# Causal attention and a top-2 expert layer: score products of two heads in the two 64-row halves of the array, and expert weights loaded early

## The reference

```python
def lora_linear(x, w, b, la, lb):
    return x @ w.T + b + 0.5 * (x @ la.T @ lb.T)
# x: (4, 512, 128), 16 heads of 8 channels, all in float32
q, k, v = split(lora_linear(x, w_attn, b_attn, la_attn, lb_attn), 3)
att = softmax(where(causal, q @ k.T / sqrt(8), -inf))          # per head
x = layernorm(x + lora_linear(att @ v, w_proj, b_proj, la_proj, lb_proj))
scores = softmax(x @ router_w)                                # 8 experts
weights, idx = top_k(scores, 2); weights /= sum(weights)
expert_e(x) = (silu(x @ gate[e]) * (x @ up[e])) @ down[e]      # 128 -> 352 -> 128
x = layernorm(x + sum_k weights[k] * expert_idx[k](x))
```

## Time and profile before

| what | us |
|---|---|
| median of 3 runs | 393.46 (392.91 to 393.8) |
| span of the profiled execution, first to last instruction | 388.3 |
| TensorE / VectorE / ScalarE / GpSimd busy | 293.4 / 233.5 / 157.7 / 184.8 |
| first row maxima (L805) | 44.9 |
| first T unit | 57.4 |
| T unit t0 of quads 1 and 2 | 68.4 and 79.8 |
| loop of three passes | 79.8 to 214.7 |
| last score product | 230 |
| first expert product (L1263) | 264.6 |

### The profile page before, as it was taken

The page is one execution under the profiler, slowest core; times in us unless marked ns, Lnnn a source line. Parts: engine busy times, 40 slices in busy tenths (PEclk is TensorE's granted clock), DMA queues, the critical chain, the costliest instruction groups (busy, mean ns, idle before and its releaser), DMA issues.

```text
span 388.3 us, 7846 instructions
## 1 busy us (share of the span) xinstructions
PE 293.4 (76%) x2082; PEld 175.3 (45%) x2101; DVE 233.5 (60%) x561; ACT 157.7 (41%) x258; POOL 184.8 (48%) x291
## 2 busy tenths in 40 slices
PE   2948568979997999989998783208999999999100
PEld 1524323424454445434455332205777777777100
DVE  7699986546687666776677203613545454555082
ACT  1324105546554566636666660011333333333014
POOL 8998623223354475446745722250444443444362
PEclk9988898989999899989999997556999999999755
DMA  6029968908100000000000129442111111111253
GB/s 148 11 101 212 254 119 292 163 4 142 26 3 3 15 29 15 1 0 22 29 8 1 31 56 356 110 117 55 40 51 58 42 49 49 54 50 38 83 145 103
DMA packets 36007, 29.97 MB, mean 77 GB/s; under 512 B 4093, under 2 KB 33920, under 8 KB 35985
## 3 DMA queue, kind: packets, MB, share of 16 engines
q1 hardware_dynamic: 32624, 24.71, 26.6%
q0 software_dynamic: 2304, 4.24, 3.2%
q10 hardware_dynamic: 1056, 0.75, 0.9%
HBM read 16.86 MB, written 13.09 MB: 77 GB/s over the span
## 4 chain that ended last, share of the span: by engine, by line
PE 53%; DVE 16%; issue 8%; DMA 7%; SPq 5%; POOL 5%; ACT 4%; POOLq 0%; ACTq 0%; DVEq 0%
PE slot L1263 13%; PE pvo L1093 7%; PE pvo L1277 7%; PE slot L1071 6%; PE slot L1054 6%; PE slot L1269 3%; SPq L353 2%; PE slot L1050 2%; DMA Qs<-mT 2%; SPq L329 2%; PE misc L1101 2%; ACT pvs L632 2%; DVE negm L805 2%; POOL rows_scratch L527 2%; DMA bqk<-in_L_attn_b_attn_dram 2%
## 5 line engine op out<-in xcount | busy, mean ns | idle before, releaser
L805 DVE TENSOR_REDUCE negm<-slot 128x2 f32<-128x1024 f32 (+2 forms) x96 | 98.8, 1041 | 44.1 <-PE slot L1054 42.4
L659 ACT ACTIVATE Pt<-slot 128x1024 f32<-128x1024 f32 (+1 forms) x96 | 84.5, 880 | 74.2 <-PE slot L1071 71.6
L503 POOL TENSOR_SCALAR_AFFINE_SELECT Pt<-Pt 128x512 f32<-128x512 f32 x56 | 35.5, 634 | 72.8 <-ACT Pt L659 72.4
L575 POOL DMA_INDIRECT chosen_scratch<-Pt x39 | 38.3, 983 | 65.8 <-ACT Pt L712 64.5
L1054 PE MATMUL slot<-Ks,Qs 128*128 (+4 forms) x254 | 57.6, 309 | 1.1 <-DVE negm L805 0.3
L1071 PE MATMUL slot<-Qs,Ks 128*128 (+4 forms) x256 | 53.0, 310 | 5.5 <-DMA Qs<-mT 4.1
L1263 PE MATMUL slot<-Ks,Pt 128*128 x156 | 54.9, 476 | 0.0
L1093 PE MATMUL pvo<-Pt,vst 128*9 128x128 f32 (+3 forms) x512 | 47.4, 450 | 0.0
L1050 PE MATMUL slot<-maskb,identb 128*128 128x128 bf16 (+1 forms) x162 | 38.8, 240 | 6.5 <-DVE negm L805 3.2
L959 DVE COPY Pt<-slot 128x256 f32<-128x256 f32 x39 | 16.5, 424 | 43.2 <-PE slot L1269 43.2
L527 POOL DMA_INDIRECT rows_scratch<-early,place x32 | 31.8, 993 | 15.2 <-issue 8.1
(11 more groups left out here) (164 smaller groups left out, 378.9 us busy)
## 6 DMA issues: line engine op xcount, KB each, us to landing
Qs<-parts_scratch SPq DMA_DIRECT2D x8, 384.0 KB, 5.9
Ks<-parts_scratch SPq DMA_DIRECT2D x8, 384.0 KB, 8.8
Pt<-rows_scratch SPq DMA_DIRECT2D x39, 65.0 KB, 1.8
Qs<-chosen_scratch SPq DMA_DIRECT2D x8, 256.0 KB, 4.9
parts_scratch<-Pt SPq DMA_DIRECT2D x4, 384.0 KB, 6.0
parts_scratch<-early SPq DMA_DIRECT2D x4, 384.0 KB, 3.2
Ks<-in_L_ffn_gate_proj_dram SPq DMA_DIRECT2D x1, 1408.0 KB, 6.8
Ks<-in_L_ffn_up_proj_dram SPq DMA_DIRECT2D x1, 1408.0 KB, 10.0
```

Of the source, the lines that this page charges most:

```text
L503: pool.affine_select(out=v, in_=v, compare_op=ALU.is_ge, fill=0.0, base=0, pattern=[[0, HQ], [1, P]], channel_multiplier=-1).then_inc(sele ...
L575: pool.indirect_dma_start(chosen_scratch, bass.IndirectOffsetOnAxis(xg[:, ring, C:C + 1].bitcast(U32), 0), ys[:, ring % OUT_RING, :], None ...
L659: act.activation(p_view(par, kb)[:, h0:h0 + heads, :], t_view(u, (2 * u + 1) % 3), ACT.Exp, scale=SCALE).then_inc(exp_done, 1)
L805: dve.tensor_reduce(negm[:, par, qb, h0:h0 + heads], s_view(u, n), AX_X, ALU.max, negate=True).then_inc(max_done, 1)
```

## The change

Score products contract one half of the array: 48 rows for S units, 51 for T units, starting at row 0 or 64. `Ks` gets the shape of `Qs`, two heads in one block, without zeros. The maxima and the ones move behind the 48 rows. In a slot, the first half of the columns (one PSUM bank) now belongs to the even heads and the second to the odd ones (`s_view`, `t_view`), so that products issued in turn for rows 0 and 64 write to different banks. The maxima and exponentials address the heads accordingly.

The mask is now made of half-height pieces too: `pick` selects the upper or the lower 64 output rows, `tri` and `tri_after` are the triangles; four products per unit, two of full and two of half block width. Their lower halves are copied by two DMAs on GpSimd's queue. The clearing of the stacks goes on both engines; the ones come by two DMAs of SyncE after the stack of batch 0.

As `Ks` is half as large, `GUW` and `DW` have memory of their own. Their five loads move from SyncE, behind the last score product, to ScalarE, behind the projections' copies and ahead of the first copy of `mT`. `vst` and its copies go; value products read `V9`. TensorE's loop over batches is written out, which makes g a constant.

```diff
 
+
+    ROWS = D * PRODUCTS
+    ALL_ROWS = ROWS + PARTS
     Q_SLOTS = ((0, 3, 0), (3, 2, 1), (5, 1, 2))
...
         onesb = sb("onesb", [P, P], BF16)
-        maskb = sb("maskb", [P, HQ, P], BF16)
-        mask_after = sb("mask_after", [P, HQ, P], BF16)
-        blank_k = sb("blank_k", [P, 2, T], BF16)
-        blank_q = sb("blank_q", [P, T], BF16)
+
+
+        pick = sb("pick", [P, 3 * HALF], BF16)
+        tri = sb("tri", [P, P], BF16)
+        tri_after = sb("tri_after", [P, P], BF16)
+        ones_rows = sb("ones_rows", [PARTS, QPB * 2 * T], BF16)
         PW = [(TB - kb) * P for kb in range(TB)]
         POFF = [HQ * sum(PW[:kb]) for kb in range(TB)]
         Pt = sb("Pt", [P, 2, HQ * sum(PW)])
...
 
-        free_k = Ks[:, :, :, :].rearrange("p g h t -> p (g h t)").bitcast(F32)
-        GUW = free_k[:, 0:2 * E * F].rearrange("p (e w f) -> p e w f", e=E, w=2)
-        DW = free_k[:, 2 * E * F:2 * E * F + E * NFC * C].rearrange("p (e k c) -> p e k c", e=E, k=NFC)
+        GUW = sb("GUW", [P, E, 2, F])
+        DW = sb("DW", [P, E, NFC, C])
         taken = [0]
 
...
-            return slot[n][:, :].rearrange("p (h k) -> p h k", k=[128, 256, 512, 512][qb])[:, 0:heads, 0:(qb + 1) * P]
+            return slot[n][:, :].rearrange("p (a c k) -> p a c k", a=2, k=[128, 256, 512, 512][qb])[:, :, 0:heads // 2, 0:(qb + 1) * P]
 
         def t_view(u, n):
             kb, _, heads = T_UNITS[u]
-            return slot[n][:, :].rearrange("p (h k) -> p h k", k=[512, 512, 256, 128][kb])[:, 0:heads, 0:PW[kb]]
+            return slot[n][:, :].rearrange("p (a c k) -> p a c k", a=2, k=[512, 512, 256, 128][kb])[:, :, 0:heads // 2, 0:PW[kb]]
 
         def p_view(par, kb):
             return Pt[:, par, POFF[kb]:POFF[kb] + HQ * PW[kb]].rearrange("p (h q) -> p h q", h=HQ)
...
 
-                sp.wait_ge(blanked[b], 1)
                 for s in range(2):
                     sp.wait_ge(parts_stored[s][b], 16 * PARTS)
                     src = parts_scratch[b, s].rearrange("(j a r) t -> a r j t", a=2, r=D * PRODUCTS)
                     for a in range(2):
-                        row = HALF * a + PARTS
-                        if s == 0:
-                            dst = Qs[row:row + D * PRODUCTS, QPB * b:QPB * (b + 1)].rearrange("p g c t -> p (g c) t")
-                        else:
-                            dst = Ks[row:row + D * PRODUCTS, QPB * b:QPB * (b + 1)].rearrange("p g (c a) t -> p a (g c) t", a=2)[:, a]
-                        sp.dma_start(dst, src[a]).then_inc(stacks_loaded, 16)
+                        stack = (Qs, Ks)[s][HALF * a:HALF * a + ROWS, QPB * b:QPB * (b + 1)].rearrange("p g c t -> p (g c) t")
+                        sp.dma_start(stack, src[a]).then_inc(stacks_loaded, 16)
 
             def store_maxrows(g, par):
 
                 sp.wait_ge(mT_copied, g + 1)
                 for h in range(HQ):
-                    sp.dma_start(Qs[HALF * (h % 2):HALF * (h % 2) + PARTS, bass.ds(g, 1), h // 2, :],
+                    row = HALF * (h % 2) + ROWS
+                    sp.dma_start(Qs[row:row + PARTS, bass.ds(g, 1), h // 2, :],
                                  mT[PARTS * h:PARTS * (h + 1), par, :]).then_inc(maxrows[par], 16)
 
 
             for b in range(2):
                 store_parts(b)
                 load_stacks(b)
+                if b == 0:
+                    sp.wait_ge(ones_ready, 1)
+                    for a in range(2):
+                        row = HALF * a + ROWS
+                        sp.dma_start(Ks[row:row + PARTS].rearrange("p (b g) c t -> p b (g c t)", b=B),
+                                     ones_rows[:, :].rearrange("p (o t) -> p o t", o=1).broadcast_to([PARTS, B, QPB * 2 * T])).then_inc(ones_loaded, 16)
             store_maxrows(0, 0)
             for b in range(2, B):
                 store_parts(b)
...
 
-            sp.wait_ge(scores_for_exp, NU * G)
-            for w, src in enumerate((gate_proj, up_proj)):
-                sp.dma_start(GUW[:, :, w, :], src.rearrange("e d f -> d e f")).then_inc(experts_loaded, 16)
-            for k, (f0, fn) in enumerate(FC):
-                sp.dma_start(DW[0:fn, :, k, :], down_proj[:, f0:f0 + fn, :].rearrange("e f c -> f e c")).then_inc(experts_loaded, 16)
-
             sp.wait_ge(fills_ready, 1)
             for e in range(0, E, 2):
...
-            pool.memset(maskb[:, :, :], 0.0).then_inc(ident0, 1)
-            pool.wait_ge(ident0, 2)
+            pool.memset(pick[:, :], 0.0).then_inc(ident0, 1)
...
-            pool.affine_select(out=maskb[:, :, :], in_=maskb[:, :, :], compare_op=ALU.is_ge, fill=NEG,
-                               base=0, pattern=[[0, HQ], [-1, P]], channel_multiplier=1).then_inc(consts_ready, 1)
+            middle = pick[:, HALF:2 * HALF]
+            pool.affine_select(out=middle, in_=middle, compare_op=ALU.not_equal, fill=1.0,
+                               base=0, pattern=[[-1, HALF]], channel_multiplier=1).then_inc(ident0, 1)
+            pool.wait_ge(ident0, 4)
+            pool.affine_select(out=middle, in_=middle, compare_op=ALU.not_equal, fill=1.0,
+                               base=-HALF, pattern=[[-1, HALF]], channel_multiplier=1).then_inc(consts_ready, 1)
+            upper = tri[0:HALF, :]
+            pool.affine_select(out=upper, in_=upper, compare_op=ALU.is_ge, fill=NEG,
+                               base=0, pattern=[[-1, P]], channel_multiplier=1).then_inc(mask_ready, 1)
             pool.wait_ge(ident_ready, 1)
             pool.tensor_copy(identb[:, :], identf[:, :]).then_inc(consts_ready, 1)
+            pool.memset(tri_after[:, :], 0.0).then_inc(ident0, 1)
+            pool.wait_ge(ident0, 5)
+            upper = tri_after[0:HALF, :]
+            pool.affine_select(out=upper, in_=upper, compare_op=ALU.is_ge, fill=NEG,
+                               base=-HALF, pattern=[[1, P]], channel_multiplier=-1).then_inc(mask_ready, 1)
+            pool.memset(ones_rows[:, :].bitcast(I32), ONE_ONE).then_inc(ones_ready, 1)
+            pool.wait_ge(mask_ready, 2)
+            for mask in (tri, tri_after):
+                pool.dma_start(mask[HALF:P, :], mask[0:HALF, :]).then_inc(masks_loaded, 16)
             pool.memset(carry[:, :], 0.0)
...
-
-            for i, b in enumerate(range(2, B)):
-                quads = slice(QPB * b, QPB * (b + 1))
-                pool.memset(Ks[:, quads].rearrange("p g h t -> p (g h t)").bitcast(I32), 0).then_inc(zeroed, 1)
-                pool.memset(Qs[:, quads].rearrange("p g c t -> p (g c t)").bitcast(I32), 0).then_inc(zeroed, 1)
-                pool.wait_ge(zeroed, 2 * i + 2)
-                for a in range(2):
-                    heads = Ks[HALF * a:HALF * a + PARTS, quads].rearrange("p g (c a) t -> p a (g c) t", a=2)[:, a]
-                    last = pool.memset(heads.bitcast(I32), ONE_ONE)
-                last.then_inc(blanked[b], 1)
-
-                pool.wait_ge(blanked[b], 1)
...
                 if end is not None:
                     inverse_deviation(end)
-                if not isinstance(g, int) or g >= 2:
-                    wait_counted(pv_done, g - 1)
-                pool.tensor_copy(vst[:, par].rearrange("p t h d -> p (t h d)"),
-                                 V9[:, bass.ds(g, 1)].rearrange("p g t h d -> p (g t h d)")).then_inc(vst_ready, 1)
                 for kb in range(TB):
                     if selects:
                         select(g, par, kb)
...
                         act.wait_ge(pv_done, g - 1)
-                    act.activation(p_view(par, kb)[:, h0:h0 + heads, :], t_view(u, (2 * u + 1) % 3), ACT.Exp,
+                    act.activation(p_view(par, kb)[:, h0:h0 + heads, :].rearrange("p (c a) q -> p a c q", a=2), t_view(u, (2 * u + 1) % 3), ACT.Exp,
                                    scale=SCALE).then_inc(exp_done, 1)
                     if u == 1 and maxrows:
                         copy_mT(g + 1, 1 - par)
...
                         exp_gap(end)
+
+            for w, src in enumerate((gate_proj, up_proj)):
+                act.dma_start(GUW[:, :, w, :], src.rearrange("e d f -> d e f")).then_inc(experts_loaded, 16)
+            for k, (f0, fn) in enumerate(FC):
+                act.dma_start(DW[0:fn, :, k, :], down_proj[:, f0:f0 + fn, :].rearrange("e f c -> f e c")).then_inc(experts_loaded, 16)
 
...
-
-            def blank(b):
-
-                for c in range(2):
-                    dve.tensor_copy(Ks[:, QPB * b:QPB * (b + 1), 2 * c:2 * c + 2, :].rearrange("p g h t -> p g (h t)"),
-                                    blank_k[:, :, :].rearrange("p (o a) t -> p o (a t)", o=1).broadcast_to([P, QPB, 2 * T]))
-                dve.tensor_copy(Qs[:, QPB * b:QPB * (b + 1)].rearrange("p g c t -> p (g c) t"),
-                                blank_q[:, :].rearrange("p (o t) -> p o t", o=1).broadcast_to([P, 2 * QPB, T])).then_inc(blanked[b], 1)
-
-            blank(0)
             dve.memset(pvo[:, :], 0.0)
             dve.memset(V9[:, :, :, :, D:D + 1], 1.0)
 
...
```

(61 more changed lines are left out.)

27 lines of the change are left out of this document (8 added, 19 removed).

## The result

The changed kernel takes 398.47 us in the median (394.63 to 399.86, 8 runs), the kernel before in the same series 394.31 (392.91 to 396.8): ratio 1.008 [1.004, 1.012]. Forecast were 376 us, range 366 to 387. A second series gave 392.84 against 388.6, ratio 1.010 [1.007, 1.014]. The profiled execution has a span of 398.0 us and its own time was 399.86, so 1.9 us lie around a span. The 5.2 us carried over in the prediction were mostly (3.3 us) an execution of the kernel before that was quicker than its median; so the two profiled spans (388.3 and 398.0) overstate the difference.

The account below looks back on a forecast made before the run. TensorE was taken to set the loop's pace, VectorE's clearing and full DMA engines to bound the prologue. Prologue -3, passes -14.1 and last quads -0.3 gave -17.4: span 388.3 to 370.9, plus 5.2 carried over, 376 us, range 366 to 387.

Parts of the forecast that it names:

- The first maxima move by -7.1: Prologue: without VectorE's clearing and with quicker casts, the chain of splits and the first maxima come 7.1 us earlier.
- With halved rate the issuing lasts from 33 to about 50: +5 us on this chain: Prologue: ScalarE's issue of expert weights delays the first mT copy, and the maxima and stores behind it, by 5 us.
- Rival 2: Prologue: DMA collision in full, quad 2 starts at 81 to 82 us; prologue +1.5, total 380.5 us, chance 0.15.
- estimate of 80 us of summed work for quad 2: Prologue: DMA start at 20 plus 28, 14, 8 and 10 us of traffic puts quad 2's t0 at 80 us.
- TensorE's loop is written out: 0: Attention loop: straight code doesn't starve TensorE, judged by the stretch of 68 to 78 us; effect 0.
- the loop, -14.1: Three attention passes: halves shorten each by 4.7 us, -14.1 in all, bounds -9 to -19.5.
- rivals 1 and 3: 1: halves overlap, short products don't, 382 us, chance 0.17; 3: halves don't run side by side, 395.7 us, chance 0.10.
- The model of gaps: Plain quad: VectorE's 6.95 us plus gaps of 0.7 and 0.75 make 8.4 us instead of 9.6.
- The third bound, the row of maxima: Plain quad: the chain from t0 until the row of maxima lands takes 7.9 us, just below 8.4.
- I take nothing off: Loop: no deduction for a lower TensorE clock, as a quad with TensorE 84% busy ran at 0.96.
- The tail: Last two quads, which have no S units and wait for exponentials and rows of maxima: halves save 0.3 us.
- Rival 5: Something else, such as rows of maxima, holds the quad: plain quad 9.1, passes -2.5 each, 383 us, chance 0.05.

Follow-up runs that it names:

- after_again: The changed kernel unaltered, timed once more in a second series: 392.84 us, 1.010 of the kernel before.
- weights_late: The changed kernel with the five expert weight loads back on SyncE's queue behind the last score product: 378.5 us, 0.975; 0.969 in another series.
- gate_up_early: weights_late with the gate and up loads issued by ScalarE in the prologue, ahead of the first copy of mT: 385.83 us, 0.991.
- late_split_first: weights_late with GpSimd's split of the maxima ahead of its last selection instead of behind it: 374.48 us, 0.9635; 0.9665 in a later series.
- before_out_split_again: The kernel before with TensorE's loop written out and GpSimd's split ahead of its last selection, timed once more: 390.77 us, 0.991.

## Why the prediction was wrong

The forecast was -17.4 us, measured were +4.2 (394.31 to 398.47). The prologue is 10 to 12 us off, the loop 8 to 9, the tail 1. Both signs of being wrong that the prediction named came: t0 of quad 2 at 86.6 and 88.8, outside 72 to 81, and passes of 44.1 and 43.3 us, above 42.5.

**The prologue's own part held.** "The first maxima move by -7.1": -8.05 and -7.0. Without the weights 6.1 of it arrive at quad 2 (74.5 against 80.6); at quad 0 only 2.6, since the rows of maxima then stand behind the second stack.

**Failed: the price of the weights.** The prediction kept -3 of -7.1, so it charged 4 us for 4.2 MB more in a stretch where the DMA engines were full. They cost 14.3 (after_again against weights_late). "With halved rate the issuing lasts from 33 to about 50: +5 us on this chain": it lasted from 33.5 to 59.0 and held the copy 14.6 us (59.0 against 44.4; 17.4 in after_again). Rival 2 had the mechanism (full engines and a blocked queue) and was priced at +1.5 with 0.15. The estimate of 80 us of summed work for quad 2 forgot that SyncE works in order: each stack load waits for its stores, and the last of these stores took 13.9 us in the changed kernel, beside the weights, and 9.8 in weights_late. The page "DMA: Bandwidth & Descriptors" of the Trainium skill, section "Queues, rings and completion order", says that the engines take turns between queues; the prediction gave the halved rate by it as its upper bound and then took less. The traces agree with the rule in the main: this store took 9.8 us in weights_late and 11.03 in late_split_first, 19.43 in gate_up_early and 13.9 in the changed kernel, 1.3 to 2 times as long beside the weights.

**Failed: "TensorE's loop is written out: 0".** It gains 2.8 us in the kernel before by the medians, 5 in the loop by the profiles. The straight stretch that the prediction looked at only showed that it does no harm. What it didn't look at are the loop's entry and turns, where the profiles put 4.6 of the 5 us; why they cost this much wasn't tried.

**Mis-sized: the loop, -14.1.** Measured -5.2 to -6.5, of which 0.2 to 1.5 go beyond the written-out loop. The first half of the mechanism was right: halves overlap, rivals 1 and 3 fell. At full clock and with the split moved the four quads are 9.58, 8.33, 10.01 and 12.69 us, sum 40.6 against a forecast of 40.3. That this fits is partly luck: from 45.0 the written-out loop, priced at 0, gives 1.6, the split 0.4, and the halves 2.4 instead of 4.7. The model of gaps was right for the plain quad (8.33 against 8.4; 1.05 us gained against 1.2). Too large were the first quad (0.7 against 1.5, which counted on a clock of 0.85 that this quad doesn't have once the loop is written out), the third (0.7 against 1.0) and the fourth (nothing against 1.0, as VectorE's work there is as long as TensorE's). The third bound, the row of maxima, adds up to 7.6 us and not 7.9, which changed nothing. Two more things kept the changed kernel from 40.6. One is GpSimd, which the prediction didn't count among those late next: TensorE waits 0.79 us in the quad shown (9.13 us) and 0.35 in its like of the next pass (8.69). The other is the clock, of which the prediction said "I take nothing off": the pass shown has a quad at 0.69 that takes 10.93, the next pass one at full clock that takes 9.69 by first exponentials. In the first pass quad 4 also waited 2.45 us for its rows of maxima, issued behind the loads of the last stack.

**The tail** was small either way: -0.3 forecast, +0.7 between the first two rows of the table. Rival 5, the rows of maxima, held in the prologue and at quad 4, not in the rest of the loop.

## What to carry to other kernels

Loads that are hidden anyway have nothing to win from an earlier place; put into a stretch with full DMA engines, they cost here by their bytes and by what the issuing engine had next, so price both and ask what stands behind each. When the full engine gets shorter, list every small hand-over (here four tiny GpSimd operations behind a selection) before crediting the gain, ask quad by quad which engine has the most work (here the fourth gained nothing), and price a loop at the lower clock too. A side edit such as a written-out loop deserves a run of its own, or its gain is credited to the main idea.

## What the hardware showed unexpectedly

- Issuing three DMAs held ScalarE for 23.0 to 27.7 us beside SyncE's traffic (four profiles), against 9.2 us on SyncE alone.
- Two products in rows 0 and 64 overlap completely: 0.38 us for two of 512 columns, 0.27 to 0.28 for four of 128. With it the granted clock is 0.90 to 0.97 over the loop, against 1.00 in the full-height kernels with the loop written out and 0.96 in the kernel before, in stretches that differ from execution to execution.
- All versions take some 6 us longer between quad 14 and the expert stage in some series. All of it lies between the first exponentials of quads 14 and 15, 8.3 to 9.1 us in one kind of series and 13.3 to 15.6 in the other, and one chip showed both kinds. In before_out_split_again TensorE has gaps there that no engine ends (2.55 us before 224.91), and ScalarE waits for something that the profile doesn't name:

```profile
224.17 3.39 ACT L659 ACTIVATE Pt<-slot 128x512 f32<-128x512 f32 x4 [4.03 <-remote]
```

Why is open. It makes a profile of one series and a median of another incomparable at this size.
